# A transformer block on one core: split down weights streamed by SyncE in three-term products, and an attention with spread projections and filler products

## The reference, cut to what matters

```
x = x + attention(layernorm(x))      # 16 heads of 16, rope, causal softmax, low-rank adapters in q, k, v, o
x = x + ffn(layernorm(x))            # 4 experts, top 1
x = x + mamba2(layernorm(x))         # unchanged by this change
x = x + ffn(layernorm(x))            # the same weights again

def ffn(x):                          # Wg, Wu: 4 x 256 x 1024, Wd: 4 x 1024 x 256
    probs = softmax(x @ Wr + br); e = argmax(probs)
    return (silu(x @ Wg[e]) * (x @ Wu[e])) @ Wd[e] * probs[e]
```

## Time and profile before

| what | value |
|---|---|
| median of 3 runs | 2193.57 us (2185.24 to 2199.95) |
| the profiled execution | 2185.0 us |
| its span | 2183.1 us |
| mean granted TensorE clock | 0.901 |
| busy: TensorE / DVE / ACT / POOL | 83% / 55% / 38% / 33% |
| moved by DMA | 161.23 MB |

### The profile page before, as it was taken

One profiled execution on the slowest core, in us unless ns is written; L12 is line 12 of the kernel. 1 busy time (PEld: TensorE's weight loads), 2 busy tenths in 40 slices (PEclk: granted clock), 3 DMA queues, 4 the chain that ended last, 5 costly groups with the idle time before them and its releaser, 6 DMA issues. The chain is left out here.

```text
span 2183.1 us, 30159 instructions
## 1 busy us (share of the span) xinstructions
PE 1819.3 (83%) x9520; PEld 1212.1 (56%) x9520; DVE 1191.3 (55%) x2979; ACT 822.7 (38%) x1705; POOL 725.6 (33%) x922
## 2 busy tenths in 40 slices
PE   5368889889888864899999658989898938999997
PEld 3133334434433322788888535747484727888886
DVE  4466676666666508543443356665656685443442
ACT  2036655656665624111111035554646441111111
POOL 2335464464462312222222124333242312222221
PEclk9569989989988855999999969999999978999999
DMA  5522333332442108000000230100101080000000
GB/s 160 174 89 90 119 126 95 122 125 77 134 135 87 39 16 313 22 24 28 26 25 26 70 111 15 43 36 1 78 1 78 1 309 22 26 24 30 25 24 9
DMA packets 90179, 161.23 MB, mean 74 GB/s; under 512 B 23080, under 2 KB 50476, under 8 KB 88880
## 3 DMA queue, kind: packets, MB, share of 16 engines
q1 hardware_dynamic: 71504, 107.39, 14.7%
q0 software_dynamic: 17984, 50.62, 7.2%
q10 hardware_dynamic: 544, 1.31, 0.2%
HBM read 102.52 MB, written 45.48 MB: 68 GB/s over the span
## 5 line engine op out<-in xcount | busy, mean ns | idle before, releaser
L690 ACT ACTIVATE a_probs<-a_ps_e 128x512 f32<-128x512 f32 (+3 forms) x768 | 336.0, 491 | 204.1 <-PE a_ps_e L854 200.9
L438 DVE CUSTOM_DVE_ANT_0 a_ps_m<-a_ps_m,a_causal 128x512 f32<-128x512 f32 (+3 forms) x512 | 239.4, 517 | 97.5 <-PE a_ps_m L841 96.4
L1433 PE MATMUL g_ps_y<-g_w_d,x_res 128*128 x1120 | 253.2, 379 | 2.8 <-DVE x_res L1203 2.8
L854 PE MATMUL a_ps_e<-a_q_st,a_k_st 64*128 64x512 f32 (+3 forms) x768 | 187.9, 480 | 76.4 <-ACT a_probs L690 48.5
L854 PEld LDWEIGHTS a_ps_e<-a_q_st,a_k_st 64*128 64x128 f32 x768 | 79.6, 201 | 289.8 <-ACT a_probs L690 200.5
L1433 PEld LDWEIGHTS g_ps_y<-g_w_d,x_res 128*128 128x128 f32 x1120 | 212.3, 190 | 34.6 <-issue 3.2
L442 DVE TENSOR_REDUCE a_peak<-a_ps_m 128x1 f32<-128x512 f32 x256 | 164.8, 686 | 94.8 <-PE a_ps_m L841 94.1
L841 PE MATMUL a_ps_m<-a_k_st,a_q_st 64*128 64x512 f32 (+3 forms) x768 | 152.7, 399 | 68.8 <-DMA a_k_st<-a_scr_k 28.0
L1323 ACT COPY x_res<-g_ps_h 128x512 f32<-128x512 f32 x70 | 41.1, 587 | 439.2 <-PE g_ps_h L1441 439.2
L576 POOL TENSOR_SCALAR_AFFINE_SELECT a_probs<-a_probs 128x256 f32<-128x256 f32 x256 | 103.9, 408 | 284.1 <-ACT a_probs L690 283.8
L1170 DVE BATCH_NORM_STATS2 g_xe_stats<-x_res 128x6 f32<-128x256 f32 x70 | 29.9, 426 | 295.6 <-DMA x_res<-g_x_rows,g_token_i 295.6
(11 more groups left out here) (272 smaller groups left out, 3664.5 us busy)
## 6 DMA issues: line engine op xcount, KB each, us to landing
a_q_st<-a_scr_q POOLq DMA_DIRECT2D x32, 512.0 KB, 4.0
a_k_st<-a_scr_k POOLq DMA_DIRECT2D x32, 512.0 KB, 4.8
m_spread_acs<-m_acs_rows SPq DMA_DIRECT2D x8, 2048.0 KB, 9.7
a_scr_q<-a_high SPq DMA_DIRECT2D x36, 256.0 KB
a_scr_k<-a_high SPq DMA_DIRECT2D x36, 256.0 KB
a_swapped<-a_raw SPq DMA_DIRECT2D x64, 128.0 KB, 2.0
g_w_gu<-L_ffn_Wg SPq DMA_DIRECT2D x8, 1024.0 KB, 9.8
g_w_gu<-L_ffn_Wu SPq DMA_DIRECT2D x8, 1024.0 KB, 12.4
```

What stands on the lines that cost most here:

```text
L438: nc.vector.tensor_tensor_reduce(ps_m[:, bank, 0:w], ps_m[:, bank, 0:w], causal[:, 512 - w:], 1.0, MASKED, ALU.add, ALU.max, peak[:, p % 2 ...
L690: nc.scalar.activation(probs[:, N % RING, r, q0:], ps_e[:, (2 * N + r) % HEAD_BANKS, q0:], ACT.Exp, scale=DH ** -0.5).then_inc(exp_done, 1)
L854: nc.tensor.matmul(ps_e[:, (2 * N + r) % HEAD_BANKS, q0:], k_st[rows(r), p % BUFS, j * P:(j + 1) * P], q_st[rows(r), p % BUFS, 512 * c + q ...
L1433: last = nc.tensor.matmul(ps_y[:, 0:D], hid_t[:, f * P:(f + 1) * P], w_d[:, bass.ds(e, 1), f].rearrange("p a d -> p (a d)"), start=(f == 0 ...
```

## The change

**Expert layer.** The down weights are no longer held in SBUF. During attention (units 12 to 15) they are split once: SyncE loads an expert (`load_down`), ACT rounds it in four pieces (`round_down`), POOL subtracts (`lower_down`), SyncE stores both parts (`store_down`) into a DRAM tensor `down_rows` in which every f-row has 256 rounded and 256 remainder columns. In the expert layer SyncE reads the expert's number of each slot and streams 2 MB for it into one of two buffers. `down` becomes 8 float32r products of 512 columns (high hidden x both parts) and 8 of 256 (low hidden x rounded part). ACT rounds the hidden rows in two copies, DVE subtracts twice, and `result` has two steps. In DVE's order stats(j+2) moves from before combine(j) to after result(j-1), and center(j+1) stands before combine(j).

**Attention.** `put_rows` moves from POOL to SyncE. q, k and v are projected in steps 2, 8, 14, 20; swaps, rotations, roundings and keeps are spread after them, into the next unit. The loads of x wait for the first pair of q and k; moments of sequence 1 lie between maxima, those of 2 and 3 in later units. At the start half of the first keeps go to ACT's queue, with buffers of their own. From step 19 of unit 14 a filler product (`keep_warm`) of 512 columns, whose result nobody reads, follows each step: 29 in all.

```diff
-    LORA_AT, XT_AT, OUT_AT, QK_AT, V_AT, LORA_O_AT = (1, 4, 9), (6, 7, 12, 13), (15, 17, 19, 21), (3, 5, 7, 9), (3, 5, 7, 9), 13
+    LORA_AT, XT_AT, OUT_AT, QK_AT, V_AT, LORA_O_AT = (1, 4, 9), (6, 7, 12, 13), (15, 17, 19, 21), (2, 8, 14, 20), (2, 8, 14, 20), 11
...
+        wd_raw = [w[:].rearrange("p i q -> p (i q)") for w in (raw, rope)]
+        wd_high = [[x_t[:, 0], x_t[:, 1]], [xn[:].rearrange("p t d -> p (t d)"), swapped[:].rearrange("p i q -> p (i q)")]]
+        wd_rows = C["wd_rows"].rearrange("(e p) (t a d) -> e p t a d", p=P, t=FF // P, a=2)
+        WD_AT = {12 * CORE + 10 + 14 * e: e for e in range(EXPERTS)}
...
+        def parts(blk, i):
+            if blk == 0 and i >= 2:
+                return first_high[:, i % 2], first_low[:, i % 2]
+            return high[:, i % 2], low[:, i % 2]
+
+        def keep(eng, blk, i):
+            eng.wait_ge(low_ready, 4 * blk + i + 1)
+            n, half = i % 2, i // 2
+            to = scr[n][blk % 2, :, :, :, half * 512:(half + 1) * 512]
+            hi, lo = parts(blk, i)
+            for c, part in enumerate(((hi, hi, None, lo), (hi, lo, None, hi))[n]):
+                if part is not None:
+                    eng.dma_start(to[:, c], part).then_inc(scr_out[i % 2], 16)
...
+            def put_rows(p):
+
+                sp.wait_ge(piece_act, ACT_NO["max", p] + 1)
+                for r in range(2):
+                    sp.dma_start(q_st[64 * r + 32:64 * r + 33, p % BUFS, :].bitcast(F32), less_t[r * T:(r + 1) * T, p % 2, :]).then_inc(rows_in[p % BUFS], 16)
...
+            def load_down(e):
+                sp.wait_ge(low_ready, 4 * 2 * BATCH)
+                if e >= 2:
+                    sp.wait_ge(wd_out, 48 * (e - 1))
+                sp.dma_start(wd_raw[e % 2].rearrange("p (t d) -> p t d", d=D), A["Wd"][e].rearrange("(t p) d -> p t d", p=P)
+                             ).then_inc(wd_in, 16)
+
+            def store_down(e):
+                sp.wait_ge(wd_less, 4 * (e + 1))
+                sp.dma_start(wd_rows[e, :, :, 1], wd_raw[e % 2].rearrange("p (t d) -> p t d", d=D)).then_inc(wd_out, 16)
+                for k in range(2):
+                    sp.dma_start(wd_rows[e, :, 4 * k:4 * k + 4, 0], wd_high[e % 2][k].rearrange("p (t d) -> p t d", d=D)
+                                 ).then_inc(wd_out, 16)
...
-            for i in range(4):
-                keep(0, i)
+            for i in (0, 2):
+                keep(sp, 0, i)
+            sp.wait_ge(pair_in[0], 32)
             for b in range(1, BATCH):
                 sp.dma_start(X[:, b * T:(b + 1) * T], x[:, b * T:(b + 1) * T]).then_inc(x_in[b], 16)
-            for i in range(4):
+            for i in range(3):
                 swap(1, i)
-            for i in range(4):
-                keep(1, i)
+            keep(sp, 1, 0)
+            put_rows(0)
+            swap(1, 3)
+            for i in (1, 2):
+                keep(sp, 1, i)
+            put_rows(1)
+            keep(sp, 1, 3)
...
+            for k in range(0, CUTS[0], 2):
+                maxima(k, k + 2)
+                if k in range(22, 22 + 2 * T, 2):
+                    row_moments(1, (k - 22) // 2)
+                if k == 42:
+                    moments(1)
...
+            def lower_down(e, k):
+                pool.wait_ge(wd_rounded, 4 * e + k + 1)
+                part = wd_raw[e % 2][:, 512 * k:512 * k + 512]
+                high_part = wd_high[e % 2][k // 2][:, 512 * (k % 2):512 * (k % 2) + 512]
+                nc.gpsimd.tensor_tensor(part.bitcast(F32R), part, high_part, ALU.subtract).then_inc(wd_less, 1)
...
-            ROPE_AT = {6: (0, 0), 7: (0, 1), 8: (0, 2), 9: (1, 0), 10: (1, 1), 11: (1, 2), 12: (2, 0), 13: (2, 1),
-                       14: (2, 2), 15: (0, 3), 17: (1, 3), 19: (3, 0), 21: (3, 1), 23: (3, 2)}
+
+            ROPE_AT = {5: (0, 0), 6: (0, 1), 7: (0, 2), 11: (1, 0), 12: (0, 3), 13: (1, 1), 14: (1, 2), 17: (2, 0),
+                       18: (1, 3), 19: (2, 1), 20: (2, 2)}
+            ROPE_THEN = {1: (3, 0), 2: (3, 1), 3: (2, 3), 4: (3, 2), 9: (3, 3)}
...
+            def round_down(e, k):
+                if k == 0:
+                    act.wait_ge(wd_in, 16 * (e + 1))
+                high_part = wd_high[e % 2][k // 2][:, 512 * (k % 2):512 * (k % 2) + 512]
+                nc.scalar.copy(high_part.bitcast(F32R), wd_raw[e % 2][:, 512 * k:512 * k + 512]).then_inc(wd_rounded, 1)
...
+            def keep_warm():
+                pe.wait_ge(chunk_max, TOTAL)
+                nc.tensor.matmul(ps_m[:, last_bank], q_st[:, (2 * UNITS - 3) % BUFS, 0:P],
+                                 k_st[:, (2 * UNITS - 3) % BUFS, 0:512], start=True, stop=True)
...
+                    if N >= 2 and issued_after(N - 2) == TOTAL:
+                        keep_warm()
...
-            for e in range(EXPERTS):
-                sp.dma_start(w_d[:, e], F["Wd"][e].rearrange("(t p) d -> p t d", p=P)).then_inc(wd_in, 16)
+            sp.wait_ge(owner_ready, 1)
+            for j in range(SLOTS):
+                if j >= 2:
+                    sp.wait_ge(y_ps, j - 1)
+                e = sp.value_load(owner_i[0:1, j:j + 1], min_val=0, max_val=EXPERTS - 1)
+                sp.dma_start(w_d[:, j % 2].rearrange("p f d -> p (f d)").bitcast(F32),
+                             by_expert[:, bass.ds(e, 1)].rearrange("p a c -> p (a c)")).then_inc(streamed[j % 2], 16)
...
-                nc.vector.tensor_copy(hid_t[:, 0:512], ps_h[:, 0]).then_inc(ht_lo, 1)
+                for c in range(2):
+                    dve.wait_ge(ht_hi, 2 * j + c + 1)
+                    some = slice(c * 512, (c + 1) * 512)
+                    nc.vector.tensor_tensor(hid_lo[:, some], ps_h[:, c], hid_hi[:, some].bitcast(F32), ALU.subtract
+                                            ).then_inc(ht_lo, 1)
...
-                nc.vector.scalar_tensor_tensor(rows[:, j % 2], ps_y[:, 0:D], scale[:, j:j + 1], xe[:, j % XE], ALU.mult,
-                                               ALU.add).then_inc(row_sb, 1)
+                step(nc.vector.scalar_tensor_tensor(rows[:, j % 2], ps_y[:, 0:D], scale[:, j:j + 1], xe[:, j % XE],
+                                                    ALU.mult, ALU.add))
+                nc.vector.scalar_tensor_tensor(rows[:, j % 2], ps_y[:, D:2 * D], scale[:, j:j + 1], rows[:, j % 2],
+                                               ALU.mult, ALU.add).then_inc(row_sb, 1)
...
-            center(1)
             weights()
             for j in range(SLOTS):
-                if j + 2 < SLOTS:
-                    stats(j + 2)
+                if j + 1 < SLOTS:
+                    center(j + 1)
                 combine(j)
                 if j == 0:
                     scales()
@@ -1223,7 +1315,7 @@
                 if j >= 1:
                     result(j - 1)
                 if j + 2 < SLOTS:
-                    center(j + 2)
+                    stats(j + 2)
...
-                nc.scalar.copy(hid_t[:, 512:1024], ps_h[:, 1]).then_inc(ht_hi, 1)
+                for c in range(2):
+                    nc.scalar.copy(hid_hi[:, c * 512:(c + 1) * 512], ps_h[:, c]).then_inc(ht_hi, 1)
...
-            def down(j, e):
-                pe.wait_ge(ht_lo, j + 1)
-                pe.wait_ge(ht_hi, j + 1)
+            def down(j):
+                w = w_d[:, j % 2]
+                pe.wait_ge(streamed[j % 2], 16 * (j // 2 + 1))
                 if j == 0:
-                    pe.wait_ge(wd_in, 16 * EXPERTS)
                     pe.wait_ge(scale_ready, 1)
                 if j >= 1:
                     pe.wait_ge(row_sb, j)
                 for f in range(FT):
-                    last = nc.tensor.matmul(ps_y[:, 0:D], hid_t[:, f * P:(f + 1) * P],
-                                            w_d[:, bass.ds(e, 1), f].rearrange("p a d -> p (a d)"), start=(f == 0),
-                                            stop=(f == FT - 1))
+                    if f % 4 == 0:
+                        pe.wait_ge(ht_hi, 2 * j + f // 4 + 1)
+                    nc.tensor.matmul(ps_y[:], hid_hi[:, f * P:(f + 1) * P], w[:, f], start=(f == 0), stop=False,
+                                     skip_group_check=True)
+                for f in range(FT):
+                    if f % 4 == 0:
+                        pe.wait_ge(ht_lo, 2 * j + f // 4 + 1)
+                    last = nc.tensor.matmul(ps_y[:, 0:D], hid_lo[:, f * P:(f + 1) * P], w[:, f, 0:D], start=False,
+                                            stop=(f == FT - 1), skip_group_check=True)
```

More of the change, by code:

```diff
@@ L593, in _ @@
                 load(p)
-            for b in range(1, BATCH):
-                inverse_std(b)
             pool.wait_ge(rope_in, 16)
@@ L707, in _ @@
                         round_high(0, i)
+                    for i in (1, 3):
+                        keep(act, 0, i)
                 if e in ACT_NO:
@@ L2112, in program @@
     with ExitStack() as ctx:
+        with ExitStack() as under:
+            hid = [under.enter_context(nc.sbuf_tensor("hidden_" + k, [P, FF], F32R)) for k in ("high", "less")]
```

(1 more changed line is left out.)

114 lines of the change are left out of this document (65 added, 49 removed).

## The result

| | median, us | lowest to highest |
|---|---|---|
| before, on the same chip | 2196.76 | 2185.24 to 2200.41 |
| after | 2171.97 | 2167.93 to 2174.43 |
| forecast | 2091 | 2045 to 2150 |

The ratio is 0.9884, with an interval of 0.9854 to 0.9914: 1.2% faster, where 4.3% were forecast. The profiled execution took 2174.43 us with a span of 2172.5 at clock 0.889, so 10.6 us less than the one before (span 2183.1, clock 0.901). The medians are 24.8 us apart: the profiled execution before was the fastest of its four, the one after the slowest of its four. What follows explains these 10.6 us, and shows some 14 us less gain than the medians.

A forecast was written before the change was run, and what follows sets the result against it. TensorE bounds the expert layers; in attention no engine is full, and waits and TensorE's low clock cost time. Terms -38 - 28 - 11 - 8 - 7 + 8 - 10 = -94 us from 2185.0 give 2091 us, range 2045 to 2150.

The forecast's parts named there:

- The expert layers: Expert slots: down falls from 3.45 to 2.90 us, 0.55 less in each of 70 slots, -38 us.
- the narrow product: Expert layer's down: each of 8 products of 256 columns takes 0.13 us; 0.108 gives -51 us, 0.2325 gives +19.
- the first two rivals: Expert slots: weight stream sets the slot, 2262 us, chance 0.06; narrow products as slow as weight load, 2126 us, chance 0.17.
- Start of attention: Attention's start: earlier loads and first scores, the 13.16 us gap and 7.33 us wait gone, -28 us (bounds 15 to 34).
- Rows by SyncE: Unit starts in attention: six waits for rows behind POOL's rotations, 13.7 us, mostly go, -11 us (bounds 5 and 14).
- Clock in the middle: Three attention units at clock 0.69: a third of the lost 50 - 42 us comes back each, -8 us (0 to 20).
- Projections spread: Nine attention units: each spread projection uses some of TensorE's waits for ACT, 0.7 us a unit, -7 us (0 to 15).
- Splitting the weights: Attention, mostly units 13 and 14: ACT's copies of down weights delay exponentials, +8 us (0 to 14).
- Filler: Attention's last unit: 29 products keep the clock up, about 28 us instead of 40, -10 us (bounds -14 and +12).
- rival of both halves failing: Whole kernel: expert layers and attention both give no gain, 2150 to 2185 us, no difference; chance 0.05.
- attention gives half: Attention: SyncE's queue or projections become the wait POOL was, filler doesn't hold clock; 28 instead of 56, 2119 us; chance 0.2.

The follow-up runs named there:

- the old steps: Changed kernel with projections back at steps 3, 5, 7, 9 and swaps, rotations, roundings, keeps where the kernel before has them: 2129.72 us (0.9717).
- POOL's order: Changed kernel with the first half's scale at step 8 of the next unit, not 23, and odd units' loads at step 10, not 14: 2141.47 us.
- the best kernel: Changed kernel with projections back at 3, 5, 7, 9, and the first half's scale moved from step 23 to step 8 of the next unit: 2106.91, again 2116.38 us.

## Why the prediction was right or wrong

**The expert layers were forecast well.** Slot 9.48 us instead of 10.12, where 9.57 was forecast: from the first silu to the last the two layers gave 22.5 and 21.8 us, 44.2 where the sum has 38. In the slot the narrow product is the term that was off, 0.1175 us instead of 0.13; the wide one measured 0.234 against 0.2325. Before the first silu and after the last, 4.8 and 2.3 us came on top, which the forecast had at nothing or at 0.5 a layer, so that the layers as wholes gave 37.2; no run takes these apart. By the rule of the Trainium skill (TensorE: Matmul & The Clock Gate, Back-to-back issue gap), which it gives for a single product by itself, both products would be 7 to 8% shorter, 2.60 us for down against 2.81 measured. Neither the stream (228 GB/s over the second stretch, no wait of `down` for it) nor weight loads of 188 ns set the pace, so the first two rivals fall.

**Start of attention, -28: got -21.6** by the end of unit 0, 18.9 of them by the scores of its second step (120.56 against 139.43 in the earlier trace rows). The gap of 13.16 us went and the 7.33 became 1.46, as forecast. The load didn't come 8 us sooner: it is issued at 66.79, where it was 66.38. My step priced the second queue at nothing. ACT's keeps stand behind its last rounding, and the three DMAs of the last one take 5.57 us to issue, up to 58.87 us; SyncE alone had ended at 60.74. From there to the load were 7.9 us, where they had been 5.6; why they grew isn't shown. So the stream of scores that resumed at 89.87 runs from 74.41, 15.5 us sooner where the forecast had 25. What the start did gain at the load was its landing, 5.4 us to the first scores instead of 9.1, with no loads of x in front.

**Rows by SyncE, -11: right in its own terms, and given back.** The six waits of 13.7 us are gone. In the same six units stands, with the old steps, the weighing's wait behind `scale`, 13.2 us in 6, and moving one scale brought 13 to 23 us. This is the rival "half, since another wait takes its place", but the queue was POOL's, not SyncE's.

**Clock in the middle, -8: not in the changed kernel.** Units 4, 8 and 12 took 53.2, 49.8 and 47.2 us, where they had 49.0, 50.1 and 49.6. With the projections together and POOL's order mended, in five profiled runs, the three take 137.8 to 148.5 us in all, where they had 148.7: between nothing and 11 us came back, 7 on average. None of these kernels waits for rows, and the three units stay long, so the rows were at most a part of what lowers the clock there.

**Projections spread, -7 with bounds of 0 to 15: the failed step.** It cost 42 us, and 25 to 35 where the scale is moved on both sides. I weighed four projections against TensorE's waits for ACT and left out three things. First, the followers: I wrote "three steps of over 1 us for a landing of two to three, tight but held", and it didn't hold. The keep of step 11 ends the chain for the load, in unit 2 at 232.79 us, and a swap that lands late stops POOL's rotation with the load behind it. Second, POOL's order: what stands behind its waits for the inverse and for a swap, 30 us with both mended, of which the scale's 13 to 23 are owed with the old steps too. The Trainium skill (Perfetto Trace Analysis, Tensor Engine Instruction) calls POOL's queue strictly first in, first out; the traces agree, as the load at 185.57 moved to 177.00 when it was put ahead of a waiting rotation. Third, whether a step is even or odd: 16 us in the medians of two pairs, 9 and 15 by the ratios, and only 7 in the profiled units 1 to 11 of one of them. In medians, the change goes 2172 (as it is), 2141 (POOL's order), 2127 (followers where they were, for which the projections moved together from six steps apart to four), 2111 (odd steps), and there it meets the kernel with all projections together and the scale moved, 2107 and 2116. The gain of 7 isn't there even then. The step that failed is "spread, each projection can use some of it": the 48.5 us of waits for ACT are 125 waits of at most 0.9 us, and a projection lasts 1.98.

**Splitting the weights, +8: nothing that can be told**, 2173.46 against 2171.97; units 12 to 15 take 154.4 and 153.6 us. Units 13 and 14 did get longer, 38.7 and 34.6 us where they had 31.6 and 30.6, but without the split they take 36.2 and 38.0; whether the loads and stores do it no run shows. **Filler, -10: -6 to -8 in the last unit**, clock 0.95 about as forecast, but 33.1 us instead of 28. The mis-sized term is the filler's own time: 0.23 us was taken, and from the start of a filler to that of the next product, where nothing else holds it, the trace has 0.42 us or more:

```profile
790.30 0.49 PE L950 MATMUL a_ps_m<-a_k_st,a_q_st 128*128 128x512 f32 x1
790.72 0.39 PE L924 MATMUL a_ps_e<-a_q_st,a_k_st 64*128 64x256 f32 x2
```

For the 24 fillers of the unit that is some 4.6 us more, an estimate from these rows. In the total the filler is not to be told.

The time is 22 us above the range because the spread's bounds were 0 and 15 us of gain, with no loss among them. (The bounds of all seven terms at once give 2037, not 2034; nothing hangs on it.) The result lies where my rival of both halves failing has its time, but not by that mechanism: the layers gave nearly all they should. It is nearer to the rival "attention gives half", whose cause, that projections become the wait, came true with a larger price. A rearrangement on four in-order queues needs a bound on the side of a loss, and nothing in the rows excluded one.

## What to carry to other kernels

Before moving a producer, follow its chain to the last consumer step by step, and list what stands behind each waiting instruction on every in-order queue: a long wait that costs nothing today (60 us at POOL) may be covered by another wait, and start to cost when that one is removed. Put extra work into the steps that hold least on the same engine, and don't count on many small waits as if they were one. Price a rearrangement with a loss as well as a gain; here the best version took the change without its new steps and moved one wait, 3.6 to 4.2% faster than before instead of 1.2%.

## What the runs showed of the hardware

Idle time cost more than its own length here, through TensorE's clock. From the best kernel to the changed one, units 1 to 11 hold the same products, but TensorE is busy 377.69 us at clock 0.98 in one and 419.06 at 0.88 in the other: of 67 us in length, 41 are the same work with more of it at the lower of its two clocks (1.2 and 2.4 GHz), and only the other 26 are idle time, 85 us instead of 59. No single wait in the changed kernel's list is above 4.3 us in that stretch. The two don't go in step, though: over units 1 to 11 kernels of this case have 59 us idle at 0.98, 66 and 76 at 0.95, 81 at 0.91 and 85 at 0.88, but also 62 at 0.94 and 71 at 0.96.

Issuing isn't free: the last three of ACT's DMAs at the start took 5.57 us to issue, 1.44 to 2.59 us each, where the three ahead of them took 0.62 to 1.18. And narrow float32r products of 256 columns follow each other at 0.1175 us with weight loads recorded at 188 ns each, so a recorded weight load is no lower bound for the pace.
